# One-hot tiles of a graph layer: the column numbers read from SBUF instead of PSUM

## The chip, the cores and the metric

The kernel runs on one core of a Trainium2 chip. The metric is the device time of one execution in microseconds (us). Three executions of the kernel before took 2099.63 to 2100.09 us, with a median of 2099.67 us.

## What is computed

One layer of a graph network with eight relations, followed by a feed-forward step on half of the nodes. There are 6250 nodes of 256 features and 206250 edges, sorted by destination. Cut to what matters here:

```python
hx  = einsum('ni,rio->rno', layernorm(x), weight)        # 8 relations
agg = segment_sum(hx[edge_type, src], dst, 6250)
x1  = x + agg * 0.7071 + h_bias + (layernorm(x) @ loop_weight) * 0.7071
out = x1 + ffn(layernorm(x1))      # ffn: top half of the nodes by x @ wr, the others pass through
```

## The kernel before, in words

The kernel sums the messages before it multiplies them by the relation weights. Edges come in 538 groups of 384 (3 tiles of 128). For each tile, GpSimd (POOL) gathers 128 rows of the normalized nodes by an indirect DMA (`gather`, line 487), which takes its row numbers from the SBUF tensor `gather_rows`. VectorE makes a one-hot tile, 128 edges by 128 columns, which says for each edge to which pair of relation and destination it belongs (`build`, line 1055; `keys` holds the column of each edge, in 16 bits). TensorE multiplies the gathered rows with the one-hot tile and so sums them by column (`sum_group`, line 796). ScalarE copies the sum out of PSUM (line 607), TensorE turns it (line 806) and VectorE adds it into a window of sums in SBUF (`add_group`, line 1137). When all groups of a block of 128 nodes are through, the block is closed: VectorE carries what hangs over into the next block's window (`carry`, line 1145, two SBUF inputs), ScalarE copies the window, and TensorE multiplies by the relation weights (lines 828, 830) and then runs the feed-forward step (lines 849, 859). VectorE's part of it is lines 1160 to 1191: the instructions of lines 1162, 1177 and 1180 have two SBUF inputs, those of lines 1172 and 1191 one tensor and scalars per partition. At the end, 49 blocks are chosen from and put out (lines 1245 to 1303).

The order of each engine's work is written out by hand. A loop over ticks goes through the groups on TensorE, ScalarE and VectorE; blocks that close put their steps in between. POOL's queue has nothing but the gathers: three for each group, two for 16 of the groups, whose last tile SyncE loads row by row. The gather of group g waits until the sum of group g - 14 is done (`RING = 14`). On VectorE's queue a build makes the tiles of two groups with one instruction (768 elements per partition). Four builds are ahead of the loop; after that, a build for groups n + 7 and n + 8 stands behind each add of an odd group n. TensorE waits for builds 0 and 1 alone (`onehot_ready`); later ones are known to be in time by the order of the queues.

The build compares `keys` with the column numbers 0 to 127. `iota0` holds them in SBUF. Before the first build, line 1062 copies them into PSUM bank 7, and all builds read that copy (`columns`). At that time the queue has behind it lines 947 and 949, the factors of the first raw rows, on which ScalarE waits for line 580; TensorE's first sum waits for line 580 and for the first build.

Early on, VectorE's lines 971 and 972 work on 1920 elements per partition with two SBUF inputs each (in line 971 one of them is broadcast along the elements), while POOL's first gathers run.

Of the kernel before, what the change touches and what calls it, by code (L numbers as in the profile page):

```python
# [25 lines left out]
P = 128  # L26
# [8 lines left out]
def gnn_ffn_program(nc, x, src, dst, edge_type, rel_w, h_bias, loop_w, wr, br, w1, b1, w2, b2, out):  # L35
# [13 lines left out]
    J = 3  # L49
    EP = 128  # L50
# [71 lines left out]
    with ctx:  # L122
        def sb(name, shape, dt=F32):
            return ctx.enter_context(nc.sbuf_tensor(name, shape, dt))

        def sem(name):
            return ctx.enter_context(nc.semaphore(name))
# [72 lines left out]
        iota0 = sb("iota0", [P, P])  # L200
# [46 lines left out]

        banks = [ctx.enter_context(nc.psum_tensor(f"bank{i}", [P, BANK], F32)) for i in range(8)]

        columns = banks[7][:, 0:P]  # L250

        pads_set = sem("pads_set")
        acc_pad_set = sem("acc_pad_set")
# [42 lines left out]
        row_step = sem("row_step")  # L296
        tables_ready = sem("tables_ready")
        sums_clear = sem("sums_clear")
        columns_ready = sem("columns_ready")
        gathered = [sem(f"gathered{i}") for i in range(RING)]  # L300
        side_rows_in = sem("side_rows_in")
        side_in = [sem(f"side_in{i}") for i in range(2)]
# [595 lines left out]
        def _(dve):  # L898
            V = nc.vector
# [152 lines left out]
            def build(q):  # L1052

                u = 2 * q % SLOTS
                built = V.tensor_tensor(onehot[0:EP, u:u + 2, :, :].rearrange("p u j c -> p (u j) c"),  # L1055
                                        columns[0:EP, :].unsqueeze(1).broadcast_to([EP, 2 * J, P]),
                                        keys[0:EP, 2 * q:2 * q + 2, :].rearrange("p g j -> p (g j)").unsqueeze(2).broadcast_to([EP, 2 * J, P]),
                                        ALU.is_equal)
                if q < 2:
                    built.then_inc(onehot_ready, 1)  # L1060

            V.tensor_copy(columns, iota0[:, :]).then_inc(columns_ready, 1)
            dve.wait_ge(columns_ready, 1)
            dve.wait_ge(slab_taken, 2 * GT)
            build(0)
            dve.wait_ge(sums_clear, 1)

# [126 lines left out]
            def routing_constants():  # L1194
# [12 lines left out]
                link(pick_step, V.memset(enough[:, DVE_DIGITS:15], float(2 * SELECTED - P * NB)))  # L1207

            build(1)
            raw_moments_of(1)  # L1210
            build(2)
            raw_factors_of(1)
            build(3)
# [114 lines left out]
```

## Time and profile before

| | us |
|---|---|
| median of 3 runs | 2099.67 |
| the profiled execution | 2100.03 |
| its span, from the first to the last instruction | 2098.4 |
| POOL busy | 1525.2 |
| TensorE busy | 1717.8 |
| VectorE busy | 793.3 |
| ScalarE busy | 734.9 |

The profile is of one execution. The span is what its rows cover; the execution's own time is 1.6 us longer. A busy share is a mean over stages. Idle time of an engine is put down to what ended it; "issue" is idle time in which the engine waited for nothing that the profile shows.

### The profile page before, as it was taken

Reading aid. Unit: us, or ns where it says so; the run is one execution under the profiler, and the core shown is the slowest. Engines: PE = TensorE matmul, PEld = TensorE weight load, DVE = VectorE, ACT = ScalarE, POOL = GpSimd, SP = SyncE. Lnnn points to the kernel's source line nnn. Section 1 sums busy time; section 2 is a strip of 40 time slices with the busy share of each in tenths; the row PEclk is TensorE's granted clock in tenths of the full one; section 3 lists DMA queues with packets and bytes.
Section 4 is the critical chain, followed back from the end, with each engine's and each line's share of the span. In section 5 each row is a group of like instructions: output and inputs, shape, how many; then the busy total and the mean of one; then the engine's idle time right before and its main releaser. Section 6 shows DMA issues by size and latency. Waiting matters only on the chain.

```text
span 2098.4 us, 30549 instructions
## 1 busy us (share of the span) xinstructions
PE 1717.8 (82%) x8696; PEld 1459.7 (70%) x8696; DVE 793.3 (38%) x1880; ACT 734.9 (35%) x1524; POOL 1525.2 (73%) x1615
## 2 busy tenths in 40 slices
PE   2796898988888788888888888888888888898883
PEld 1585687767776677777667767767777777777773
DVE  8743343343333334233432333343333334333337
ACT  6733333333332333242333323332422333333242
POOL 7777777777777777777777777777777777777730
PEclk9998899999999999999999999999999999999995
DMA  8953433433433433433433343433333343343336
GB/s 326 325 162 107 127 105 110 124 107 107 126 106 107 125 107 107 126 107 106 125 109 106 116 117 107 117 115 107 117 116 106 116 117 107 112 122 105 105 89 219
DMA packets 126310, 265.88 MB, mean 127 GB/s; under 512 B 32206, under 2 KB 72957, under 8 KB 126138
## 3 DMA queue, kind: packets, MB, share of 16 engines
q0 software_dynamic: 76704, 209.56, 34.3%
q1 hardware_dynamic: 37002, 42.02, 6.1%
q10 hardware_dynamic: 12432, 12.32, 1.8%
q8 instruction: 69, 1.13, 0.2%
q14 instruction: 103, 0.84, 0.1%
HBM read 244.53 MB, written 19.25 MB: 126 GB/s over the span
## 4 chain that ended last, share of the span: by engine, by line
POOL 51%; issue 18%; PE 15%; SPq 6%; DMA 5%; DVE 3%; ACT 2%; DVEq 0%; ACTq 0%; POOLq 0%
POOL messages L487 50%; PE bank L796 5%; PE bank L828 4%; SPq L428 4%; DMA messages<-normed_table,gather_rows 3%; PE bank L859 2%; PE bank L849 2%; SPq L418 1%; DMA closed<-in_x 1%; DVE acc L1303 1%; ACT hidden L655 1%; PE bank L806 1%; DMA normed_table<-closed 1%; PE bank L830 0%; SPq L425 0%
## 5 line engine op out<-in xcount | busy, mean ns | idle before, releaser
L487 POOL DMA_INDIRECT messages<-normed_table,gather_rows x1550 | 1474.0, 951 | 472.2 <-issue 461.5
L796 PE MATMUL bank<-messages,onehot 128*128 128x256 f32 x3196 | 836.2, 398 | 314.2 <-DMA messages<-normed_table,gather_rows 240.9
L796 PEld LDWEIGHTS bank<-messages,onehot 128*128 128x128 f32 x3196 | 581.0, 196 | 424.9 <-DMA messages<-normed_table,gather_rows 282.9
L1137 DVE SCALAR_TENSOR_TENSOR sums<-bank,regular,sums 128x256 f32 x538 | 260.0, 483 | 1215.3 <-PE bank L806 1174.1
L607 ACT ACTIVATE stage<-bank 128x256 f32<-128x256 f32 x538 | 206.6, 384 | 1286.6 <-PE bank L796 1273.0
L828 PE MATMUL bank<-rel_sb,closed 128*128 128x256 f32 x1568 | 356.8, 381 | 0.1
L828 PEld LDWEIGHTS bank<-rel_sb,closed 128*128 128x128 f32 x1568 | 299.2, 191 | 42.2 <-issue 0.8
L1055 DVE TENSOR_TENSOR onehot<-bank,keys 128x768 f32<-128x768 f32 x269 | 254.7, 947 | 1.2 <-issue 1.2
L806 PE MATMUL bank<-ident,stage 128*128 128x128 f32 x1076 | 209.0, 276 | 3.6 <-ACT stage L607 3.2
L859 PE MATMUL bank<-w_sb,hidden 128*128 128x256 f32 x784 | 198.4, 410 | 11.2 <-ACT hidden L655 11.1
L849 PEld LDWEIGHTS bank<-normed_t,w_sb 128*128 128x128 f32 x1568 | 200.7, 207 | 3.1
L849 PE MATMUL bank<-normed_t,w_sb 128*128 128x128 f32 x1568 | 201.3, 291 | 0.0
L859 PEld LDWEIGHTS bank<-w_sb,hidden 128*128 128x128 f32 x784 | 162.0, 209 | 43.8 <-ACT hidden L655 18.0
L806 PEld LDWEIGHTS bank<-ident,stage 128*128 128x128 f32 x1076 | 149.3, 143 | 46.9 <-ACT stage L607 4.9
L655 ACT ACTIVATE hidden<-bank,b_col 128x128 f32<-128x128 f32 x392 | 113.3, 389 | 0.6
L620 ACT ACTIVATE sums<-zero 128x2304 f32<-128x2304 f32 x49 | 103.7, 2116 | 0.0
L615 ACT ACTIVATE closed<-sums 128x1024 f32<-128x1024 f32 x98 | 98.7, 1068 | 2.7 <-DVE sums L1145 2.7
L655 ACT ACT_TABLE_LOAD x49 | 62.9, 1283 | 0.9
L640 ACT ACT_TABLE_LOAD x48 | 61.6, 1283 | 0.9
L487 POOL DMA_INDIRECT messages<-in_x,gather_rows x48 | 48.4, 1008 | 16.8 <-issue 14.0
L830 PE MATMUL bank<-loop_sb,normed_x_t 128*128 128x256 f32 x196 | 58.3, 379 | 0.0
L830 PEld LDWEIGHTS bank<-loop_sb,normed_x_t 128*128 128x128 f32 x196 | 37.2, 190 | 5.1
(163 smaller groups left out, 587.3 us busy)
## 6 DMA issues: line engine op xcount, KB each, us to landing
side<-normed_table SPq DMA_DIRECT2D x2048, 1.0 KB
messages<-normed_table,gather_rows POOLq DMA_INDIRECT x1550
acc<-in_x SPq DMA_DIRECT2D x12, 512.0 KB, 12.6
residual<-resid ACTq DMA_DIRECT2D x12, 512.0 KB
node_out<-acc SPq DMA_DIRECT2D x12, 512.0 KB
normed_x<-normed_table ACTq DMA_DIRECT2D x11, 512.0 KB, 4.2
messages<-residual SPq DMA_DIRECT2D x6, 896.0 KB, 10.3
rel_sb<-in_L_gnn_weight SPq DMA_DIRECT2D x2, 1024.0 KB, 8.8
```

Source lines behind the costliest of these rows:

```text
L487: pool.indirect_dma_start(messages[0:EP, g % RING, j * D:(j + 1) * D], None, x if g < RAW else table, bass.IndirectOffsetOnAxis(ap=gather_ ...
L607: nc.scalar.activation(stage[:, g % STAGES, :], banks[g % STAGES][:, 0:D], ACT.Copy).then_inc(staged, 1)
L615: nc.scalar.activation(closed[:, of, :], sums[:, of, (b & 1) * OPEN:(b & 1) * OPEN + P], ACT.Copy).then_inc(closed_ready, 1)
L620: nc.scalar.activation(sums[:, :, (b & 1) * OPEN:(b & 1) * OPEN + OPEN], zero[:, 0:1].unsqueeze(1).broadcast_to([P, KR, OPEN]), ACT.Copy). ...
L655: last = nc.scalar.activation(hidden[:, m, :], banks[5 + m // 4][:, m % 4 * P:(m % 4 + 1) * P], ACT.Gelu_apprx_tanh, bias=b1_col[:, m:m + 1])
L796: last = nc.tensor.matmul(banks[g % STAGES][:, 0:D], onehot[0:EP, g % SLOTS, j, :], rows, start=(j == 0), stop=(j == J - 1))
L806: last = nc.tensor.transpose(banks[TURNS[g % 2]][:, k * P:(k + 1) * P], stage[:, g % STAGES, k * P:(k + 1) * P], ident[:, :])
L828: nc.tensor.matmul(banks[4][:, 0:D], closed[:, k * R + r, :], rel_sb[:, k, r * D:(r + 1) * D], start=(k == 0 and r == 0), stop=False)
L849: last = nc.tensor.matmul(banks[5 + m // 4][:, m % 4 * P:(m % 4 + 1) * P], w1_sb[:, k, m * P:(m + 1) * P], normed_t[:, k, :], start=(k == ...
L859: last = nc.tensor.matmul(banks[5][:, 0:D], hidden[:, m, :], w2_sb[:, m, :], start=(m == 0), stop=(m == HC - 1))
L1055: built = V.tensor_tensor(onehot[0:EP, u:u + 2, :, :].rearrange("p u j c -> p (u j) c"), columns[0:EP, :].unsqueeze(1).broadcast_to([EP, 2 ...
L1137: V.scalar_tensor_tensor(sums[:, :, to], banks[TURNS[g % 2]][:, 0:D].rearrange("p (n m) -> p n m", m=W), regular[:, 0:1], sums[:, :, to], ...
```

## The change

The builds read `iota0` in SBUF. The view of PSUM bank 7, the semaphore, the copy and the wait for it are taken out. Each build then has both of its tensor inputs in SBUF.

```diff
-        columns = banks[7][:, 0:P]
...
-        columns_ready = sem("columns_ready")
...
                 built = V.tensor_tensor(onehot[0:EP, u:u + 2, :, :].rearrange("p u j c -> p (u j) c"),
-                                        columns[0:EP, :].unsqueeze(1).broadcast_to([EP, 2 * J, P]),
+                                        iota0[0:EP, :].unsqueeze(1).broadcast_to([EP, 2 * J, P]),
                                         keys[0:EP, 2 * q:2 * q + 2, :].rearrange("p g j -> p (g j)").unsqueeze(2).broadcast_to([EP, 2 * J, P]),
                                         ALU.is_equal)
                 if q < 2:
                     built.then_inc(onehot_ready, 1)
 
-            V.tensor_copy(columns, iota0[:, :]).then_inc(columns_ready, 1)
-            dve.wait_ge(columns_ready, 1)
             dve.wait_ge(slab_taken, 2 * GT)
             build(0)
```

## Rows read from the trace of the kernel before

**Rows 1.** The page's head, its busy times, and the chain by engine.
```profile
span 2098.4 us, 30549 instructions
...
PE 1717.8 (82%) x8696; PEld 1459.7 (70%) x8696; DVE 793.3 (38%) x1880; ACT 734.9 (35%) x1524; POOL 1525.2 (73%) x1615
...
POOL 51%; issue 18%; PE 15%; SPq 6%; DMA 5%; DVE 3%; ACT 2%; DVEq 0%; ACTq 0%; POOLq 0%
```
**Rows 2.** Costliest groups: gathers, builds (out<-in, count, busy us, mean ns, idle before).
```profile
L487 POOL DMA_INDIRECT messages<-normed_table,gather_rows x1550 | 1474.0, 951 | 472.2 <-issue 461.5
...
L1055 DVE TENSOR_TENSOR onehot<-bank,keys 128x768 f32<-128x768 f32 x269 | 254.7, 947 | 1.2 <-issue 1.2
```
**Rows 3.** By stage, line 487: stretch, its us, POOL busy (instructions), clock, DMA, GB/s.
```profile
375.00:675.00 300.00, 227.19 (x240) 0.97 0.39 112
```
**Rows 4.** POOL's waits from 75 to 2016 us: in total, times, longest.
```profile
POOL messages L487 <- issue: 460.3, 1511, 0.3
POOL messages L487 <- PE bank L796: 10.7, 35, 0.3
```
**Rows 5.** POOL in order of time: the last gather (start, us, idle before).
```profile
2014.34 0.95 POOL L487 DMA_INDIRECT messages<-normed_table,gather_rows  x1 [0.31 <-issue]
```
**Rows 6.** VectorE (DVE) in order of time around 57 us.
```profile
56.92 0.29 DVE L1062 COPY bank<-iota 128x128 f32<-128x128 f32 x1
57.25 0.96 DVE L1055 TENSOR_TENSOR onehot<-bank,keys 128x768 f32<-128x768 f32 x1
```
**Rows 7.** TensorE's waits, whole span.
```profile
PE bank L796 <- ACT messages L580: 32.4, 1, 32.4
```
**Rows 8.** VectorE in order of time, 13 to 18 us.
```profile
13.44 2.16 DVE L971 TENSOR_TENSOR acc<-acc,hidden 128x1920 f32<-128x1920 int32 x1
15.63 2.16 DVE L972 SCALAR_TENSOR_TENSOR acc<-acc 128x1920 f32<-128x1920 int32 x1
```
**Rows 9.** POOL in the same stretch.
```profile
13.72 2.70 POOL L487 DMA_INDIRECT messages<-in_x,gather_rows  x1 [0.30 <-issue]
16.73 1.89 POOL L487 DMA_INDIRECT messages<-in_x,gather_rows  x1 [0.30 <-issue]
```
**Rows 10.** VectorE in order of time near 1913 us.
```profile
1913.60 0.42 DVE L1145 TENSOR_TENSOR sums<-sums 128x256 f32<-128x256 f32 x1
```
**Rows 11.** POOL in the same stretch.
```profile
1913.65 1.18 POOL L487 DMA_INDIRECT messages<-normed_table,gather_rows  x1 [0.30 <-issue]
```
**Rows 12.** VectorE in order of time near 918 us.
```profile
918.63 0.45 DVE L1177 TENSOR_TENSOR resid<-x,normed 128x256 f32<-128x256 f32 x1
```
**Rows 13.** POOL in the same stretch.
```profile
918.63 0.95 POOL L487 DMA_INDIRECT messages<-normed_table,gather_rows  x1 [0.30 <-issue]
```
**Rows 14.** VectorE in order of time, 810 to 821 us.
```profile
810.00 0.95 DVE L1055 TENSOR_TENSOR onehot<-bank,keys 128x768 f32<-128x768 f32 x1
...
819.23 0.95 DVE L1055 TENSOR_TENSOR onehot<-bank,keys 128x768 f32<-128x768 f32 x1
...
820.55 0.35 DVE L1191 TENSOR_SCALAR acc<-acc,w_all 128x256 f32<-128x256 f32 x1
```
**Rows 15.** POOL in the same stretch.
```profile
810.68 0.95 POOL L487 DMA_INDIRECT messages<-normed_table,gather_rows  x1 [0.30 <-issue]
...
819.43 0.95 POOL L487 DMA_INDIRECT messages<-normed_table,gather_rows  x1 [0.30 <-issue]
820.68 1.04 POOL L487 DMA_INDIRECT messages<-normed_table,gather_rows  x1 [0.30 <-issue]
```
**Rows 16.** Line 1258: durations in ns (min/median/max), first and last start.
```profile
L1258 DVE TENSOR_TENSOR routing<-routing x8: 669/670/672, 2039.8 to 2065.7; 128x490 f32<-128x490 f32 x8
```
**Rows 17.** VectorE in order of time: the third and the last of the builds.
```profile
65.24 0.93 DVE L1055 TENSOR_TENSOR onehot<-bank,keys 128x768 f32<-128x768 f32 x1
...
1994.72 0.94 DVE L1055 TENSOR_TENSOR onehot<-bank,keys 128x768 f32<-128x768 f32 x1
```
**Rows 18.** POOL in order of time: the one gather that waited.
```profile
61.90 0.94 POOL L487 DMA_INDIRECT messages<-in_x,gather_rows  x1 [0.79 <-PE bank L796]
```

## The prediction, before the changed kernel was seen

> **What bounds the kernel now.** I read four views in this order. The page's chain that ended last comes first: half of the span is the gathers of line 487 on GpSimd (POOL), and 18% is "issue", time in which an engine waits for nothing that the profile shows [rows 1]. The reader is to see that TensorE has more busy time than POOL but holds only 15% of the chain. The second view is the costliest groups: 1550 gathers of 951 ns, with 472 us of idle time in front of them, nearly all of it "issue", that is 0.30 us for each gather [rows 2]. So a gather takes 0.95 + 0.30 = 1.25 us. The third is POOL by stage: 300 us hold 240 gathers, which is 1.25 us each with nothing left over [rows 3]. The fourth is POOL's waits: from 75 us to the last gather it waits for TensorE 35 times, for 10.7 us, longest 0.3 us [rows 4]. That is the same 0.30 us step, put down to another cause. POOL therefore runs at its own pace from start to end, and the last gather starts at 2014.34 us [rows 5], with 84 us of tail behind it. Whatever lengthens a gather moves the end by as much.
>
> **What the change touches.** The one-hot build (line 1055, 269 times 947 ns [rows 2]) and the copy in front of the first build (line 1062, 0.29 us [rows 6]). VectorE is busy for 38% of the span [rows 1] and nobody waits for a build after the first, so a build some ns longer or shorter costs nothing by itself. The question is what a build with both inputs in SBUF does to POOL.
>
> **The removed copy and its wait.** The copy starts at 56.92 us, and the first build stands behind it. TensorE's first sum waits last for ScalarE's normalized rows (line 580), not for the build [rows 7], and that step depends on VectorE's line 949, which the code has ahead of the copy. So it is worth 0, with ScalarE's work as the cover; were the cover gone, it would be worth at most 0.3 us.
>
> **The build's new operand, and how the trace shows the price.** Other VectorE instructions of this kernel have two SBUF inputs already. The longest are lines 971 and 972, which run from 13.44 to 15.60 us and from 15.63 to 17.79 us [rows 8]. The gathers that start while they run take 2.70 and 1.89 us instead of 0.95 [rows 9]. The first VectorE instruction ends 1.88 us after its gather's start, the second 1.06 us after: both gathers end 0.82 to 0.83 us after the VectorE instruction does. The same holds in the steady state: line 1145 (sums with sums, both in SBUF) runs from 1913.60 to 1914.02 us [rows 10], and the gather that starts at 1913.65 us takes 1.18 us [rows 11], which is 0.37 us to the end of line 1145 and 0.81 us more. A gather undisturbed takes 0.946 us, so the first 0.125 us of overlap is free and the rest is added to the gather one for one. Of all gathers after 75 us, 56 take over 0.98 us, 8.4 us too long in sum, and each of them starts under a VectorE instruction with two SBUF inputs or under a tensor-with-scalar one of lines 1172 and 1191.
>
> Who starts first matters. Line 1177 starting in the same 10 ns as a gather takes 0.45 us and leaves that gather at 0.95 us [rows 12, 13]. The latest start that still delays is the one just shown, 0.05 us ahead of the gather.
>
> Today's build, with one input in PSUM, does none of this. The build from 810.00 to 810.95 us lies over the start of the gather at 810.68 us, that from 819.23 us over the gather at 819.43 us, and both gathers take 0.95 us; the next gather takes 1.04 us under line 1191 [rows 14, 15]. I laid all builds over all gathers: in 146 cases the build alone covers the gather's first 0.125 us, and all 146 gathers take 0.94 or 0.95 us. In the changed kernel the build joins the other class.
>
> The Trainium skill says of this, in "SBUF — State Buffer", section "Who interferes with whom", that a VectorE instruction with two SBUF inputs contends with a GpSimd instruction that reads SBUF and not with one that only writes it. "Perfetto Trace Analysis", section "DMA Instruction — SWDGE (GPSIMD)", says that DMA instructions of GpSimd "do not read a tensor". Together they would make the change free, 2100 us. The lengthened gathers speak against the second sentence for a gather that takes its row numbers from SBUF.
>
> **The size.** A two-input instruction of 490 elements takes 670 ns [rows 16] and one of 1920 takes 2.16 us [rows 8], so 768 elements take 670 + 278 x 1.04 = 959 ns. Call o the time from a build's start to the next gather's start. For o over 0.05 the delay is 0.959 - o - 0.125 = 0.834 - o, if that is positive. The two builds above would cost 0.834 - 0.68 = 0.15 us and 0.834 - 0.20 = 0.63 us. Only one gather can be hit by a build, since the next starts 1.25 us later.
>
> There are 267 builds that count, from 65.24 us to 1994.72 us [rows 17]. The first two, before the gather at 61.90 us, are free: that gather waits 0.79 us for TensorE's first sum, 0.48 us over the step [rows 18].
>
> Two ways to add up. Spread evenly over the 1.25 us, a build costs 0.784 x 0.784 / 2 / 1.25 = 0.246 us, and 267 make 66 us. Laid over the gathers as they stand in the trace of before, 148 of the 267 delay a gather, for 61 us. Against the first, 46 of the builds follow directly on a sum that waited for its gather; they keep a fixed distance to the gathers and cost only 0.08 us each, while the other 218 that can be sorted cost 0.26 us each. A slower POOL makes TensorE wait oftener, so this group grows a little, and I take 60 us. What holds VectorE up while a gather has started first is 0.03 to 0.07 us a time, beside the path.
>
> Sum: the profiled execution took 2100.0 us (span 2098.4 us [rows 1], 1.6 us around it); its time lies 0.4 us above the median of 2099.67 us. 2100.0 - 0 (copy) + 60 = 2160 us.
>
> Bounds: were two thirds of the builds of the cheap kind, 178 x 0.08 + 89 x 0.26 = 38 us, and the time 2138 us. Shifting all builds against the gathers by -0.6 to 0.6 us gives 52 to 80 us; the upper end with 2 us for the sum's other terms gives 2182 us.
>
> **Rivals.** (1) No port is shared between this compare and the gather, because one input is 16 bit and both are broadcast, or by the two sentences of the skill. Then only the copy's 0.3 us is at stake and the time is 2099.7 us, not slower. For it: that none of the 146 covered gathers is longer today. Against: today's input lies in PSUM, and line 971 has a broadcast input too and delays its gather by 1.75 us. It decides if gathers under a build stay at 0.95 us. Chance 0.05, of which 0.02 stands for a gain of over 0.2%, from a start of the sums that I have misread.
> (2) The slack hides it: 14 groups of gathers are in flight, and were TensorE the true limit, half of the 60 us would be taken up, 2130 us. For it: TensorE is busy 82% of the span [rows 1]. Against: POOL never waits for it beyond the step [rows 4]. Chance 0.05.
> (3) Builds settle into a bad distance to the gathers. At 0.39 us each, the mean over builds that all hit, 267 make 105 us, 2205 us. For it: the builds follow from the gathers. Against: the group that follows closest is the cheap one. Chance 0.05.
>
> **How the numbers follow.** The forecast has 0.85. About 0.2%, 4.2 us, is what a measurement of this kernel can tell from no change. Faster 0.02, same 0.03, slower 0.95. The range 2138 to 2182 us takes the bounds; rivals 1 to 3 lie outside it with 0.15 in all.
>
> **What would show it.** Right: POOL's gathers of line 487 keep their minimum of 942 ns but average about 951 + 60000/1550 = 990 ns, with some 150 more of them over 0.98 us; each ends 0.82 us after a build; 300 us hold 233 gathers, not 240; the build takes 0.95 to 0.96 us, or up to 1.03 us where a gather came first; the last gather starts near 2074 us; the tail stays at 84 us. Wrong: gathers of 0.95 us under builds, or a last gather that is late by less than the gathers' added time, or POOL waiting for TensorE by more than 0.3 us at a time.

## The result, and the profile after

The changed kernel takes 2159.72 us (median of 4 runs, 2156.89 to 2162.34) against 2099.88 us of the kernel before on the same chip (4 runs). The ratio is 1.0285, with a 95% interval of 1.0272 to 1.0298: slower by 60 us. Forecast were 2160.0 us, with a range of 2138 to 2182 us. Lines of the changed file stand two to four below those of before: the gather is line 485, the build 1053, the carry 1141, TensorE's sum 794.

The page of the changed kernel, its head, the chain by engine and the groups of gathers and builds (they answer to [rows 1, 2]):

```profile
span 2157.5 us, 30547 instructions
...
POOL 53%; issue 18%; PE 14%; SPq 6%; DMA 5%; DVE 3%; ACT 1%; POOLq 0%; DVEq 0%; ACTq 0%
...
L485 POOL DMA_INDIRECT messages<-normed_table,gather_rows x1550 | 1533.9, 990 | 472.1 <-issue 460.3
...
L1053 DVE TENSOR_TENSOR onehot<-iota,keys 128x768 f32<-128x768 f32 x269 | 255.9, 951 | 1.4 <-issue 1.4
```

The mean gather went from 951 to 990 ns while the idle time in front of the gathers stayed at 472 us. That makes up the change: 1550 x 39 ns = 60 us. The build itself gained 4 ns.

The changed kernel's line 485 by stage (columns as in [rows 3]) and POOL's waits from 75 to 2080 us ([rows 4]):

```profile
375.00:675.00 300.00, 229.23 (x233) 0.96 0.38 109
```

```profile
POOL messages L485 <- issue: 459.4, 1508, 0.3
POOL messages L485 <- PE bank L794: 11.9, 39, 0.3
```

There are 233 gathers in 300 us where there were 240, and POOL still waits for nobody beyond its 0.30 us step.

Three builds of the changed kernel in order of time, VectorE first and then POOL (start, us):

```profile
604.18 0.95 DVE L1053 TENSOR_TENSOR onehot<-iota,keys 128x768 f32<-128x768 f32 x1
...
685.81 1.01 DVE L1053 TENSOR_TENSOR onehot<-iota,keys 128x768 f32<-128x768 f32 x1
...
1900.52 0.95 DVE L1053 TENSOR_TENSOR onehot<-iota,keys 128x768 f32<-128x768 f32 x1
```

```profile
604.39 1.56 POOL L485 DMA_INDIRECT messages<-normed_table,gather_rows  x1 [0.30 <-issue]
...
685.84 0.95 POOL L485 DMA_INDIRECT messages<-normed_table,gather_rows  x1 [0.30 <-issue]
...
1900.55 1.73 POOL L485 DMA_INDIRECT messages<-normed_table,gather_rows  x1 [0.30 <-issue]
```

The first build ends at 605.13 us, 0.74 us after the start of its gather; 0.74 + 0.82 = 1.56 us is what that gather takes. The second build starts only 0.025 us ahead of its gather by the profile. Here the gather goes first: it keeps its 0.95 us, and the build takes 1.01 instead of 0.95 us. The third build starts 0.03 us ahead and already holds its gather, which takes 1.73 us.

Over the whole trace, 132 builds lengthen a gather by more than 0.02 us. All of them start at least 0.029 us ahead of it; behind a lead of 0.027 us or less every gather keeps its 0.95 us. Worked out from the builds' ends, these gathers should be 62.3 us longer, and 61.9 us are found; taken one by one, each agrees to within 0.011 us. After 75 us, 183 gathers take over 0.98 us where it was 56, and they are 67.6 us too long where it was 8.4 us: 128 under builds with 61.0 us, 55 under other VectorE instructions with 6.6 us.

The last gather of the changed kernel ([rows 5]):

```profile
2074.93 0.95 POOL L485 DMA_INDIRECT messages<-normed_table,gather_rows  x1 [0.30 <-issue]
```

It starts 60.6 us later than before, the tail behind it is 82.6 us instead of 84.0 us, and the span is 59.1 us longer.

### The profile page after: what moved, and what is told of

Same layout as the page of the kernel before. It is cut to its first block, busy times and chain, and to the rows that moved or that the text cites. A ratio compares the mean times of both kernels' runs of the same rounds, so it can differ in the third digit from the quotient of the medians.

```text
span 2157.5 us, 30547 instructions
## 1 busy us (share of the span) xinstructions
PE 1747.8 (81%) x8696; PEld 1478.8 (69%) x8696; DVE 800.1 (37%) x1879; ACT 736.8 (34%) x1524; POOL 1584.5 (73%) x1615
## 4 chain that ended last, share of the span: by engine, by line
POOL 53%; issue 18%; PE 14%; SPq 6%; DMA 5%; DVE 3%; ACT 1%; POOLq 0%; DVEq 0%; ACTq 0%
POOL messages L485 53%; PE bank L794 6%; SPq L426 4%; DMA messages<-normed_table,gather_rows 3%; PE bank L826 3%; PE bank L857 2%; SPq L416 1%; DMA closed<-in_x 1%; PE bank L847 1%; DVE acc L1299 1%; PE bank L804 1%; DMA normed_table<-closed 1%; SPq L423 0%; PE bank L828 0%; ACT hidden L653 0%
## 5 line engine op out<-in xcount | busy, mean ns | idle before, releaser
L485 POOL DMA_INDIRECT messages<-normed_table,gather_rows x1550 | 1533.9, 990 | 472.1 <-issue 460.3
L794 PE MATMUL bank<-messages,onehot 128*128 128x256 f32 x3196 | 861.0, 408 | 343.9 <-DMA messages<-normed_table,gather_rows 285.3
L794 PEld LDWEIGHTS bank<-messages,onehot 128*128 128x128 f32 x3196 | 594.5, 200 | 463.1 <-DMA messages<-normed_table,gather_rows 334.2
L1053 DVE TENSOR_TENSOR onehot<-iota,keys 128x768 f32<-128x768 f32 x269 | 255.9, 951 | 1.4 <-issue 1.4
```

The lines of the kernel that those rows point to most:

```text
L485: pool.indirect_dma_start(messages[0:EP, g % RING, j * D:(j + 1) * D], None, x if g < RAW else table, bass.IndirectOffsetOnAxis(ap=gather_ ...
L794: last = nc.tensor.matmul(banks[g % STAGES][:, 0:D], onehot[0:EP, g % SLOTS, j, :], rows, start=(j == 0), stop=(j == J - 1))
```

## The experiments

The theory under test: a VectorE instruction with two SBUF inputs holds a gather that starts under it until the instruction ends, so the price depends on the number and the length of such instructions. Rivals were the removal of the copy and its wait, a sharing in proportion to the elements read, the order of the two inputs, and VectorE's queue. Kernels of one group below ran on one chip with their own runs of the kernel before: 2100.46 us for the first four, 2100.5 us for the next four, 2102.72 us for the last two.

**Copy kept, builds from SBUF.** The edit, against the kernel before:

```diff
-                                        columns[0:EP, :].unsqueeze(1).broadcast_to([EP, 2 * J, P]),
+                                        iota0[0:EP, :].unsqueeze(1).broadcast_to([EP, 2 * J, P]),
```

> The builds read the column numbers in SBUF, but the copy into PSUM bank 7 and the wait for it stay, unused. Theory (a compare with two SBUF inputs holds up a gather that starts under it, to its own end): 2160 us, within 5 us of the changed kernel, and gathers of 990 ns on average. Rival (the lost copy, its wait or the start of the sums moved the order of things): 2100 us.

Measured: 2165.98 us, ratio 1.0307 (1.029 to 1.0325), mean gather 994 ns:

```profile
L487 POOL DMA_INDIRECT messages<-normed_table,gather_rows x1550 | 1541.3, 994 | 472.4 <-issue 462.4
```

The operand alone makes the time. This kernel is 6 us above the changed one, just beyond the 5 us expected, so both were run again side by side (the last two below).

**Every second build from SBUF.**

```diff
-                                        columns[0:EP, :].unsqueeze(1).broadcast_to([EP, 2 * J, P]),
+                                        (iota0 if q % 2 else columns)[0:EP, :].unsqueeze(1).broadcast_to([EP, 2 * J, P]),
```

> Every second build reads SBUF, the others the copy in PSUM. Theory: half of the builds, half of the added time, 2100 + 30 = 2130 us, with long gathers under the SBUF builds alone. Rival (all or nothing: one such build is enough to shift the gathers against VectorE for good): 2160 us or 2100 us.

Measured: 2133.59 us, ratio 1.0157 (1.014 to 1.0173), 33 us for half of the builds. The two kinds side by side in this kernel, VectorE and then POOL:

```profile
636.05 0.95 DVE L1055 TENSOR_TENSOR onehot<-bank,keys 128x768 f32<-128x768 f32 x1
...
640.82 0.95 DVE L1055 TENSOR_TENSOR onehot<-iota,keys 128x768 f32<-128x768 f32 x1
```

```profile
636.10 0.94 POOL L487 DMA_INDIRECT messages<-normed_table,gather_rows  x1 [0.30 <-issue]
...
641.32 1.26 POOL L487 DMA_INDIRECT messages<-normed_table,gather_rows  x1 [0.30 <-issue]
```

The build from PSUM starts 0.05 us ahead of a gather and lies over nearly all of it, and the gather takes 0.94 us. The build from SBUF ends 0.45 us into its gather, which takes 0.45 + 0.81 = 1.26 us. Over this trace, 73 builds from PSUM start 0.03 us or more ahead of a gather and reach more than 0.125 us into it, and none of these gathers takes longer than 0.95 us; 79 builds from SBUF lengthen theirs, by 33 us in sum. The price follows the operand, build by build.

**Small builds, from SBUF.** One build per group, against the changed kernel; `build` itself, which is given the first group and the number of groups, is left out here.

```diff
-                    if n % 2 == 1 and n + AHEAD < NG:
-                        build((n + AHEAD) // 2)
+                    if n + SLOTS < NG:
+                        build(SLOTS, n + SLOTS, 1)
```

> One build per group (384 elements) behind each add, instead of one per two groups; all in SBUF, no copy. The same number of elements is compared. Theory (the hold lasts for the instruction, so the price grows with the square of its length): a build takes 670 - 106 x 1.04 = 560 ns, the window is 0.56 - 0.125 - 0.05 = 0.385 us, 0.385 x 0.385 / 2 / 1.25 = 0.059 us each, 530 of them 31 us: 2131 us. Rival (the two share the way to SBUF in proportion to the elements read): 2160 us.

**Big builds, from SBUF.** One build per four groups, also against the changed kernel.

```diff
-                    if n % 2 == 1 and n + AHEAD < NG:
-                        build((n + AHEAD) // 2)
+                    if n % 4 == 3 and n + 5 < NG:
+                        build(SLOTS, n + 5, 4)
```

> One build per four groups (1536 elements) in the loop, in SBUF, no copy; the first four builds stay as they are. Theory: a build takes 670 + 1046 x 1.04 = 1.76 us, longer than the gathers' 1.25 us step, so each one hits a gather, which starts 0.05 to 1.30 us after it and waits 1.63 us less that: 0.96 us on average, 132 of them 126 us and 1 to 2 us for the first four: 2227 us. Rival (sharing in proportion to the elements): 2160 us.

Measured: 2136.89 us for the small ones, ratio 1.0177 (1.016 to 1.0194), and 2228.66 us for the big ones, ratio 1.0624 (1.0603 to 1.0644). The gathers and builds on the page of the small builds:

```profile
L485 POOL DMA_INDIRECT messages<-normed_table,gather_rows x1550 | 1508.9, 974 | 472.2 <-issue 455.4
...
L1054 DVE TENSOR_TENSOR onehot<-iota,keys 128x384 f32<-128x384 f32 (+1 forms) x534 | 297.3, 557 | 1.3 <-issue 1.3
```

and of the big ones:

```profile
L485 POOL DMA_INDIRECT messages<-normed_table,gather_rows x1550 | 1599.8, 1032 | 472.1 <-issue 458.1
...
L1054 DVE TENSOR_TENSOR onehot<-iota,keys 128x1536 f32<-128x1536 f32 (+1 forms) x137 | 236.5, 1726 | 1.2 <-issue 1.2
```

One big build in order of time, VectorE and then POOL:

```profile
619.25 1.75 DVE L1054 TENSOR_TENSOR onehot<-iota,keys 128x1536 f32<-128x1536 f32 x1
```

```profile
619.56 2.25 POOL L485 DMA_INDIRECT messages<-normed_table,gather_rows  x1 [0.30 <-issue]
```

All three kernels compare the same elements, and VectorE's time for it even falls from 297 to 237 us. Yet the added time goes up with the length of one build: 36 us at 0.56 us, 60 us at 0.95 us, 128 us at 1.73 us. A sharing by elements is out. The big build above ends 1.44 us into its gather, which takes 1.44 + 0.81 = 2.25 us. Of the 137 big builds 135 lengthen a gather, by 132 us in sum; of the 534 small ones 161 do, by 40 us. The gathers too long under other instructions fall in both kernels, from 8.4 to about 4 us. The small builds cost 5 us more than expected, because the working let a build delay only from 0.05 us ahead of a gather on: with the 0.03 us of the changed kernel's trace, the same working gives 0.405 x 0.405 / 2 / 1.25 x 530 = 35 us instead of 31.

**Inputs exchanged.** Against the changed kernel.

```diff
-                                        iota0[0:EP, :].unsqueeze(1).broadcast_to([EP, 2 * J, P]),
                                         keys[0:EP, 2 * q:2 * q + 2, :].rearrange("p g j -> p (g j)").unsqueeze(2).broadcast_to([EP, 2 * J, P]),
+                                        iota0[0:EP, :].unsqueeze(1).broadcast_to([EP, 2 * J, P]),
```

> The changed kernel with the two inputs of the build exchanged: first the keys, second the column numbers, both in SBUF. Theory (two inputs in SBUF, in whichever order): 2160 us. Rival (it depends on which of them is the second input, or on the 16-bit one being there): 2100 us.

Measured: 2162.95 us in one run, mean gather 991 ns. It makes no difference which of the two is the second input.

**Small and big builds, from the copy in PSUM.** The edits are those of the small and the big builds, made to the kernel before.

> One build per group (384 elements), column numbers from the copy in PSUM: the control of the small builds. Theory: 2100 us, no gather is longer under a build, VectorE's extra 269 instructions are hidden. Rival (the number of builds itself costs): over 2110 us.

> One build per four groups (1536 elements), column numbers from the copy in PSUM: the control of the big builds. Theory: 2100 us. Rival (a long build delays the adds behind it on VectorE's queue, and so TensorE): over 2110 us.

Measured: 2099.27 us and 2100.7 us, one run each. The gathers on the two pages, small builds first:

```profile
L487 POOL DMA_INDIRECT messages<-normed_table,gather_rows x1550 | 1473.6, 951 | 472.2 <-issue 461.6
```

```profile
L487 POOL DMA_INDIRECT messages<-normed_table,gather_rows x1550 | 1474.1, 951 | 472.3 <-issue 460.4
```

Both have the 951 ns of the kernel before. Neither 265 builds more nor builds of 1.72 us on VectorE's queue cost anything as long as one input lies in PSUM.

**Four more of VectorE's instructions, their row block moved to PSUM.** Two of them have two SBUF inputs, two are tensor-with-scalar. Against the kernel before; where the code said `x1[:, :]` it now says `x1`, and a wait orders line 1160 behind the last use of the area.

```diff
-        x1 = sb("x1", [P, D])
...
         columns = banks[7][:, 0:P]
+        x1 = banks[7][:, P:P + D]
...
                 dve.wait_ge(agg_ready, b + 2)
+                if 0 < b < NB - 1:
+                    dve.wait_ge(ffn_done, 2 * b + 1)
...
-                V.tensor_tensor(acc[:, b, :], banks[5][:, 0:D], b2_b[:, :], ALU.add).then_inc(ffn_done, 1)
+                V.tensor_tensor(x1, banks[5][:, 0:D], b2_b[:, :], ALU.add).then_inc(ffn_done, 1)
...
-                V.tensor_scalar(acc[:, b, :], acc[:, b, :], w_all[:, b:b + 1],
+                V.tensor_scalar(acc[:, b, :], x1, w_all[:, b:b + 1],
```

> The kernel before, with VectorE's block of rows x1 in PSUM bank 7 instead of SBUF, also as the place between lines 1189 and 1191: the instructions of lines 1162 and 1177 then have one SBUF input, those of lines 1172 and 1191 none but their scalars. Theory: of the 56 gathers over 0.98 us in the kernel before, 41 lie under these four lines, 5.4 us in sum; they go, and those under lines 1145 and 1180 stay (15, 3.0 us): 2099.9 - 5.4 = 2094.5 us, 0.26% faster. Rival (the gather's delay is not the path, or PSUM's own cost on VectorE takes its place): 2100 us or more.

Measured: 2094.3 us (6 runs) against 2100.5 us (10 runs), ratio 0.9971 (0.9959 to 0.9983). This version is faster than both kernels. Its gathers on the page, and line 1179 (before: 1177) with its durations in ns (min/median/max):

```profile
L487 POOL DMA_INDIRECT messages<-normed_table,gather_rows x1550 | 1467.1, 947 | 472.2 <-issue 459.1
```

```profile
L1179 DVE TENSOR_TENSOR resid<-bank,normed x49: 424/424/425, 115.6 to 2030.0; 128x256 f32<-128x256 f32 x49
```

The mean gather fell to 947 ns. After 75 us, 7 gathers are left over 0.98 us, 1.2 us in sum, and all of them start under the two instructions left with two SBUF inputs, the carry and line 1180. None is over 0.98 us under the four that were changed, though in 54 cases those start 0.03 us or more ahead of a gather and reach more than 0.125 us into it. Line 1177 was held up where a gather came first (0.45 us in [rows 12]); now all 49 take 424 or 425 ns. The gain of 6.2 us is 0.8 us more than expected. Fewer of the instructions left over met a gather, 7 with 1.2 us where 15 with 3.0 us had been expected to stay; how they come to lie against the gathers was not forecast, so this part is luck. It was not free on VectorE: the tensor-with-scalar instruction of line 1172 went from 449 to 543 ns on average. VectorE is not the path, so that does not show.

**Both again, side by side.** The changed kernel and the one with the copy kept.

> The changed kernel once more, beside the next run on the same chip. The kernel with the copy kept took 6 us more than the changed kernel did on another day. Theory: chance, from how the builds happen to lie against the gathers: this kernel within 3 us of the next one, 2160 to 2166 us. Rival (keeping the copy costs 6 us, or dropping it gains them): 6 us below the next one.

> The kernel with the copy kept once more, beside the run above. Theory: within 3 us of it. Rival: 6 us above it.

Measured: 2167.86 us, ratio 1.0315 (1.0301 to 1.0329), and 2168.39 us, ratio 1.0314 (1.03 to 1.0328). The medians differ by 0.5 us, so the rival's 6 us are not there; each interval is 3 us wide to either side, and a worth of the copy of a few us cannot be excluded. Both lie above the 2160 to 2166 us expected. On this chip the same changed kernel took 65 us more than before, and its own runs spread over 13 us (2158.15 to 2171.27), where the kernel before spreads over 2.4 us; a difference of 6 us between two results is within that. Where the profiled executions differ, the builds' hits differ with them: builds lengthen gathers by 61.0 us in the execution of 2158.15 us and by 61.9 us in that of 2159.17 us, but by 67.6 us in that of 2168.44 us and by 67.8 us in that of 2167.52 us. The first two are of the changed kernel and the last two of the one with the copy kept. No execution of the changed kernel above 2160 us has a profile, so that its own spread has the same cause is argued, not shown.

## Why the prediction was right

**The bound.** Right. POOL runs at its own pace, and what a gather gains in length the end gains: +59.3 us in the duration of all 1598 gathers, +60.6 us at the last one's start, +59.1 us in the span. The slack of 14 groups took up nothing, so the second rival falls.

**The price of one build.** Right to 0.01 us, once a build holds its gather; the lead that it needs was taken too long, 0.05 us instead of 0.03. That a build with two SBUF inputs would do to a gather what lines 971 and 1145 do was the step on which all rested, and the half-and-half kernel shows it within one trace. A gather waits for a build with two SBUF inputs and not for one with a single SBUF input, while both builds write to SBUF: what differs, and holds the gather, is VectorE's second read of SBUF. That the part of the gather that waits is its own read of the row numbers is inferred; no run changes where these lie. The two sentences of the Trainium skill, taken together, would have left 2100 us. The Trainium skill's "Perfetto Trace Analysis", section "DMA Instruction — SWDGE (GPSIMD)", with its "do not read a tensor", does not fit these gathers. The Trainium skill's "SBUF — State Buffer", section "Who interferes with whom", agrees with the builds of every run here once the gather is counted among the instructions that read SBUF.

**Number and sum.** The sum was right, 60 us forecast and 59.8 us measured, but the closeness is partly luck. Forecast were 148 hits over the old gathers, worth 61 us, corrected to 60; 132 lengthened a gather, by 61.9 us. Nine of these have a lead between 0.03 and 0.05 us, which the working left out, and cost 7 us; laid over the old gathers with 0.03 us, it would have given 66 us. Terms that the sum put at nothing brought the total down again. Gathers were 2.6 us shorter outside the builds' hits, most of it under the other VectorE instructions (6.6 us after 75 us where it was 8.4 us); POOL's wait for the first sum grew by 1.3 us; the tail fell by 1.4 us. Together, 61.9 - 2.6 + 1.3 - 1.4 = 59.2 us, against 59.1 us in the span. Of some 150 more gathers over 0.98 us that were forecast, 127 came. The 38 us of the lower bound are 37 by its own terms, which changes nothing. Whether the group of cheap builds grew, for which 1 us had been taken off, stays open. The repeat with 65 us lies inside the range as well.

**The copy.** Forecast at 0, and the two kernels side by side show no difference beyond their spread. In the profiled execution, POOL's one wait for TensorE's first sum grew from 0.79 us [rows 18] to 2.08 us:

```profile
62.47 0.94 POOL L485 DMA_INDIRECT messages<-in_x,gather_rows  x1 [2.08 <-PE bank L794]
```

The gathers before it came 0.7 us sooner and the first sum 0.6 us later, so the gather behind the wait starts at 62.47 us against 61.90 us. The first sum ends at 62.2 us here and at 62.4 us in both profiles with the copy kept, so the lost copy is not what delays it.

**The tail** was forecast at 84 us and is 82.6 us. In the profiles of all kernels here it lies between 82.3 and 84.0 us, whether the builds read SBUF or PSUM, so the difference is not the change's.

**Rivals.** The first (no effect) falls with every SBUF kernel, the third (105 us) by the 132 hits at 0.47 us each: half of the builds hit, not all.

## What to carry to other kernels

When GpSimd's gathers set the pace, list the VectorE instructions with two SBUF inputs and the tensor-with-scalar ones on SBUF (some 10 of the 56 gathers over 0.98 us in the kernel before start under lines 1172 and 1191), and put an input into PSUM; a plain copy of a constant there paid 60 us here, and the row block in PSUM another 6 us. What cannot be moved should be short: the added time went from 36 to 128 us as the same work was cut into fewer, longer instructions. The price can be read before any change is made, by laying such instructions over the gathers' rows and looking for gathers that end a fixed 0.82 us after them.

## What the runs showed of the hardware that I had not expected

The hold is not alike on the two sides. A build keeps a gather waiting until its own end (2.25 us under a build of 1.75 us), while a gather that comes first keeps a build for only 0.06 us (1.01 instead of 0.95 us), although it goes on for 0.95 us. The Trainium skill's "SBUF — State Buffer", section "SBUF: two separate sides", says that the one that starts first has the pair "for the whole instruction"; that agrees for VectorE, and not for the gather against an instruction with two SBUF inputs. And the delay is exact: of the 132 gathers that builds lengthen, not one is off the rule by more than 0.011 us.

The tensor-with-scalar instructions behave otherwise. Line 1172 in the kernel before (durations in ns, min/median/max):

```profile
L1172 DVE TENSOR_SCALAR normed<-x,moments,rstd x49: 410/412/639, 115.6 to 2036.1; 128x256 f32<-128x256 f32 x49
```

Where it starts 0.42 to 0.51 us after a gather's start, it ends 0.11 to 0.12 us after the gather does and takes 0.55 to 0.64 us; where it starts up to 0.40 us after one, it takes 0.41 us. So a gather that comes first does hold this kind of instruction, by a later part of its own time.
